# Causal masks of the second attention: added by VectorE to the diagonal blocks in PSUM, in place of products of bf16 mask rows

## The reference, cut to what matters

```python
scores = jnp.einsum('bhqd,bhkd->bhqk', q, k) * scale
causal = jnp.tril(jnp.ones((s, s), dtype=bool))
scores = jnp.where(causal, scores, -jnp.inf)
attn = jax.nn.softmax(scores, axis=-1)
ctx = jnp.einsum('bhqk,bhkd->bhqd', attn, v)
```

## Time and profile before

| what | us |
|---|---|
| median of 3 runs | 4223.27 |
| lowest and highest run | 4217.36, 4226.44 |
| the profiled execution | 4211.02 |
| span of its records | 4209.2 |
| busy in the span: PE | 3110.0 (74%) |
| PEld | 1905.6 (45%) |
| DVE | 2081.5 (49%) |
| ACT | 1452.4 (35%) |
| POOL | 588.3 (14%) |

### The profile page before, as it was taken

The page is one execution under the profiler, slowest core; times in us unless marked ns, Lnnn a source line. Parts: engine busy times, 40 slices in busy tenths (PEclk is TensorE's granted clock), DMA queues, the critical chain, the costliest instruction groups (busy, mean ns, idle before and its releaser), DMA issues. The chain is left out here.

```text
span 4209.2 us, 51448 instructions
## 1 busy us (share of the span) xinstructions
PE 3110.0 (74%) x17850; PEld 1905.6 (45%) x17850; DVE 2081.5 (49%) x3955; ACT 1452.4 (35%) x2880; POOL 588.3 (14%) x814
## 2 busy tenths in 40 slices
PE   2368879999999626999944559798344317999997
PEld 1134445555555323444433438788222214666664
DVE  3278766666666443333335558122555464333333
ACT  2246655555555422333343320000333222222222
POOL 2222115555555200000000000000100000000000
PEclk7679989999999858999965555667565558999998
DMA  1122200000000020000011123310000000000000
GB/s 57 54 54 37 42 26 4 4 4 4 4 4 1 18 67 19 14 14 5 0 46 33 51 74 101 86 45 15 4 0 0 0 0 15 15 7 7 7 7 20
DMA packets 145623, 101.46 MB, mean 24 GB/s; under 512 B 42616, under 2 KB 132587, under 8 KB 145115
## 3 DMA queue, kind: packets, MB, share of 16 engines
q1 hardware_dynamic: 145464, 99.35, 8.7%
HBM read 68.69 MB, written 30.63 MB: 24 GB/s over the span
## 5 line engine op out<-in xcount | busy, mean ns | idle before, releaser
L2320 ACT ACTIVATE f_silu<-f_g 128x512 f32<-128x512 f32 x256 | 152.9, 597 | 523.1 <-PE f_u L2298 523.1
L1274 DVE TENSOR_TENSOR x_hg<-x_h,x_g_ps 128x512 f32<-128x512 f32 x248 | 170.6, 688 | 328.9 <-PE x_y_ps L1219 296.9
L936 ACT ACTIVATE a_p<-a_s_ps,a_nmax 128x512 f32<-128x512 f32 (+3 forms) x512 | 268.1, 542 | 128.1 <-DVE a_nmax L852 128.1
L2345 DVE TENSOR_TENSOR f_act<-f_silu,f_u 128x512 f32<-128x512 f32 x256 | 176.1, 688 | 264.7 <-ACT f_silu L2320 264.7
L852 DVE TENSOR_REDUCE a_nmax<-a_s_ps 128x2 f32<-128x1024 f32 (+3 forms) x256 | 205.1, 822 | 168.9 <-PE a_s_ps L753 165.4
L1259 ACT ACTIVATE x_h<-x_h_ps,x_w 128x512 f32<-128x512 f32 x256 | 175.8, 687 | 323.6 <-PE x_g_ps L1215 296.2
L2297 PE MATMUL f_g<-hsT,f_wg 128*128 (+1 forms) x512 | 264.1, 597 | 28.9 <-DMA f_wd<-in_wd 17.0
L1211 PE MATMUL x_h_ps<-x_anT,x_w 128*128 128x512 f32 x512 | 263.1, 597 | 25.1 <-DMA x_gT<-gT_d 24.5
L910 POOL TENSOR_SCALAR a_p<-a_p,a_rden 128x512 f32<-128x512 f32 (+3 forms) x512 | 264.0, 536 | 12.1 <-DVE a_rden L859 11.9
L2298 PE MATMUL f_u<-hsT,f_wu 128*128 (+1 forms) x512 | 262.3, 594 | 0.0
L1219 PE MATMUL x_y_ps<-x_hg,x_w 128*128 128x512 f32 x496 | 253.1, 592 | 0.0
(11 more groups left out here) (408 smaller groups left out, 5522.8 us busy)
## 6 DMA issues: line engine op xcount, KB each, us to landing
l_band<-in_fir_long SPq DMA_DIRECT2D x16, 768.0 KB, 4.5
parts_d<-p_parts SPq DMA_DIRECT2D x16, 384.0 KB, 2.5
a_qs<-parts_d SPq DMA_DIRECT2D x96, 64.0 KB
a_ks<-parts_d SPq DMA_DIRECT2D x96, 64.0 KB
x_w<-in_w SPq DMA_DIRECT2D x8, 514.0 KB, 8.8
chan_d<-q_nT SPq DMA_DIRECT2D x16, 256.0 KB
p_xs<-in_x SPq DMA_DIRECT2D x8, 256.0 KB, 3.1
xfT_d<-p_xfT SPq DMA_DIRECT2D x8, 256.0 KB
```

What stands on the lines that cost most here:

```text
L936: last = nc.scalar.activation(p[g % 4][:, h, c:c + width(i)], s_ps[g % 2][:, h, c:c + width(i)], ACT.Exp, bias=nmax[g % 4][:, col], accum_ ...
L2345: nc.vector.tensor_tensor(act[s][:, f, :], g[f % 2][:, :], u_ps[f % 2][:, :], ALU.mult)\
```

## The change

In `scores` the products of mask rows are gone, and the last product of q and k signals `s_done`. In `maxima` VectorE adds the fp32 mask to each diagonal block of the step, in place in PSUM, for both heads with one instruction (128 partitions by 2 x 128 elements, the mask read twice by a stride of 0). A new semaphore `masked` counts these additions, and VectorE waits for its own additions before it takes the maxima. A pair has four additions (one, two and one in its steps) and three such waits; `MASKED` has the running count. Nothing else differs, and the first attention (`attn0`) keeps its products of mask rows.

```diff
--- before.py
+++ after.py
@@ -651,6 +651,7 @@
     n_pairs = NPAIR * B
     steps = 3 * n_pairs
     BLOCKS = (((3, 0),), ((2, 0), (0, 3 * P)), ((1, 0),))
+    MASKED = (1, 3, 4)
     with ExitStack() as ctx:
         sb = lambda name, shape, dt=F32: ctx.enter_context(nc.sbuf_tensor("a1_" + name, shape, dt))
         ps = lambda name, shape: ctx.enter_context(nc.psum_tensor("a1_" + name, shape, F32))
@@ -679,7 +680,7 @@
         s_done, max_ready, exp_done, rden_ready = sem("s_done"), sem("max_ready"), sem("exp_done"), sem("rden_ready")
         p_ready, pT_done, e_ready = sem("p_ready"), sem("pT_done"), sem("e_ready")
         ctx_done, cx_ready, o_done, oT_ready = sem("ctx_done"), sem("cx_ready"), sem("o_done"), sem("oT_ready")
-        y_done, acc_ready = sem("y_done"), sem("acc_ready")
+        y_done, acc_ready, masked = sem("y_done"), sem("acc_ready"), sem("masked")
         block = ctx.enter_context(nc.Block())
         halves = [slice(h * D1, (h + 1) * D1) for h in range(2)]
 
@@ -745,14 +746,8 @@
                 after(pe, exp_done, g - 1)
                 for at, (i, c) in enumerate(BLOCKS[g % 3]):
                     for h, hh in enumerate(halves):
-                        nc.tensor.matmul(out[:, h, c:c + width(i)], qT[s][hh, i * P:(i + 1) * P], kT[s][hh, 0:width(i)],
-                                         start=(at == 0), stop=False, skip_group_check=True)
-                for i, c in BLOCKS[g % 3]:
-                    for z in range(2):
-                        for h, hh in enumerate(halves):
-                            last = nc.tensor.matmul(out[:, h, c + i * P:c + width(i)], st["halfb"][hh, 0, z, :],
-                                                    st["halfb"][hh, 1, z, :], start=False, stop=z == 1,
-                                                    skip_group_check=True)
+                        last = nc.tensor.matmul(out[:, h, c:c + width(i)], qT[s][hh, i * P:(i + 1) * P], kT[s][hh, 0:width(i)],
+                                                start=(at == 0), stop=True, skip_group_check=True)
                 last.then_inc(s_done, 1)
 
             def transposes(g):
@@ -848,6 +843,10 @@
 
             def maxima(g):
                 v.wait_ge(s_done, g + 1)
+                for i, c in BLOCKS[g % 3]:
+                    diagonal = s_ps[g % 2][:, :, c + i * P:c + width(i)]
+                    nc.vector.tensor_tensor(diagonal, diagonal, bc(st["maskf"][:, 0, :], 2), ALU.add).then_inc(masked, 1)
+                v.wait_ge(masked, NB * (g // 3) + MASKED[g % 3])
                 for at, (i, c) in enumerate(BLOCKS[g % 3]):
                     last = nc.vector.tensor_reduce(nmax[g % 4][:, 2 * at:2 * at + 2], s_ps[g % 2][:, :, c:c + width(i)],
                                                    AX.X, ALU.max, negate=True)
```

## The result

The changed kernel takes 4237.94 us (median of 6 runs), the kernel before 4221.10 us (median of 6 in the same comparison). The ratio is 1.0042, with a 95% interval of 1.0029 to 1.0055: slower by 12 to 23 us. The forecast was 4238.

The account below looks back on a forecast made before the run. The prediction took a loop through several engines, not TensorE alone, as the bound: 11.94 to 12.22 us per pair. Repeating pairs +14.6, outputs -3.5 and ends +4 make +15 us, 4223.3 + 15 = 4238 us, range 4222 to 4270.

Parts of the forecast that it names:

- The bound: Per pair, two chains meet at step 1's exps: through the copy of v 11.94 us, through VectorE's maxima 11.72 us.
- chain of the copy: Loop through ScalarE's copy of v, which waits for v's projection: 11.94 us per pair, forecast to become 11.41.
- Step 1's additions: Two VectorE additions and a wait, less an earlier start, make step 1's maxima 0.76 + 0.04 - 0.09 = 0.71 us later.
- The removed products: TensorE's mask products: step 0's worth 0.21 us on both chains, step 1's 0.32 on the copy's only, step 2's nothing.
- VectorE's chain: Loop through VectorE's maxima of step 1: 11.72 us per pair, forecast 11.72 + 0.71 - 0.21 = 12.22 us.
- Steps 0 and 2 at nothing: One addition and wait each, 0.46 us on VectorE, covered by idle time and so costed at nothing.
- The wait: VectorE waiting for its own additions: next starts 0.04 us after the end, against 0.08 earlier without a wait.
- The outputs: Seven pairs that compute a sequence's output: TensorE's products count there, about -0.5 us each, -3.5 us together.
- The ends: First pairs and last four, where VectorE's chain stands bare: 0.5 to 0.8 us each, +4 us for both ends.
- The sum: Whole stage: 52 pairs +14.6 us, outputs -3.5, ends +4, together +15 us on the median of 4223.3.
- Rival D: TensorE's clock falls after 1.9 us idle per pair, 1.6 us a fall, giving 4266 to 4280 us; chance 0.20.
- Rivals A to C: TensorE's chain decides, 4192 or 4210 us, chance 0.06; a tie, 4224, 0.17; additions at upper end, 4268, 0.07.

Follow-up runs that it names:

- e1: Changed kernel with step 1's mask products back on TensorE, VectorE adding masks in steps 0 and 2 only; 4207.2 us, 0.9979 of the kernel before.
- e2: Changed kernel with VectorE adding step 0's mask only, steps 1 and 2 by products; 4213.3 us, 0.9989 of the kernel before.
- e4: Changed kernel with the additions left out too, so no causal mask in this attention; 4195.0 us, 0.9941 of the kernel before.
- e3: Changed kernel with VectorE adding step 1's two masks only, steps 0 and 2 by products; 4237.9 us, 1.0045 of the kernel before.
- e5: Changed kernel with step 1's two additions joined into one instruction of 128x512; 4244.9 us, one run.
- e6: Changed kernel with one mask addition and wait more, in step 0, 1 or 2 in turn; 4245.0, 4315.3 and 4244.5 us, one run each.
- e9: Changed kernel with one more wait, between step 1's two independent additions; 4286.3 us, one run.
- run 48: Not a label: "the one run 48 us slower" means e9's single run, 4286.3 us, with 48 a number of microseconds.

## Why the prediction was right

**The bound.** Two chains that meet at the exps of step 1, the one through the copy of v ahead by 0.22 us: shown. e1, e2 and e4 run on the chain of the copy, the changed kernel, e3, e5 and e6 on VectorE's. e1's one pair away from the outputs without a projection of v took 11.61 us beside its 11.83, the same 0.22.

**Step 1's additions: +0.71 forecast.** The parts, in the rows of the changed kernel: two additions and the wait from 915.81 to 916.59 are 0.78 us (0.80 forecast, 0.76 and 0.04), and the first starts 0.08 after the start of the reciprocal, at +3.19 and not +3.24 as taken, so it is a gain of 0.14 on the maxima's +3.33 (0.09 forecast). In all 0.64, so the forecast's 0.71 was 0.07 too high.

**The removed products: 0.21 for step 0, 0.32 for step 1.** These are the terms that were mis-sized; 0.11 and 0.22 were right. VectorE's chain shows the 0.11 by itself, in the pair just named: 11.72 before, 11.61 in e1. 0.64 - 0.11 = 0.53 on VectorE's chain of 11.72 gives 12.25, which was measured. The forecast's 12.22 is so close because two errors of 0.07 and 0.10, one on either side, nearly cancelled. In the chain through the copy of v nothing cancelled them: 11.94 - 0.11 - 0.22 = 11.61 is what e4 took, where the forecast had 11.41.

**Steps 0 and 2 at nothing.** Shown for a pair by e2 and by e6 in both steps.

**The wait: 0.12.** Measured at 0.13 (e9).

**The outputs: -0.5 each.** Measured -0.31, and not from the steps that were forecast. e3, without step 1's products, has 18.76 for 18.99, so these give 0.23. e2, without step 0's, has the same 18.98: they give nothing there. e1, without step 2's as well, has 18.90, which is the other 0.08. Why step 0's give nothing is argued, not shown: `values` waits for the addition of the output there (e6), behind the rotation of q, which step 2's products delay.

**The ends: +4 us.** Too low. The last four distances grew from 43.7 to 48.3 us, and the start, from the first projection to the first copy of `values`, by some 3.5 more, so 8 in all. Part is TensorE's clock, which now falls three times in the last pairs where it fell once; one of the three:

```profile
1430.73 1.09 PE L761 MATMUL a_pt_ps<-ident,a_p 128*128 128x128 f32 x4 [3.43 <-ACT a_e L945]
...
1431.75 2.08 PE L749 MATMUL a_s_ps<-a_kT,a_qT 64*128 64x512 f32 x4
```

These are the transposes after 3.43 us of idle time and the scores, 2.08 us for 1.13.

**The sum.** In the two profiled executions the stage grows by 52 x 0.30 = 15.7, less 2.2 for the outputs, plus 8 at the ends, 21.5 us, where 15 was forecast; the medians say 17 (12 to 23). The stage's growth was right to within some 6 us. That the total of 4238 came out to the tenth is luck: the three runs behind the 4223.3 that the sum started from lie 2.2 us above the median of six, and the errors in the terms cancelled in part.

**Rival D.** It was held at 0.20 and priced at 1.6 us a fall. The changed kernel is free of it: in mid-stage the clock stays at 1.00. But the mechanism is there at the price given, 14.3 - 12.72 = 1.6 us. My idle time of 1.9 us was too high, since it added the products at 0.74; by what they were worth (0.11 for each of steps 0 and 2, the latter from e1's and e2's idle times, and 0.22 for step 1) it is 0.90 + 0.30 + 0.44 = 1.64 us. In these profiles 1.65 us in each pair never brought a fall in mid-stage, and 1.77 did in half the pairs. Of e9's falls 28 are in mid-stage; with these, at 1.6 us each, the changed kernel would have taken about 4238 + 45 = 4283 us, outside the range. So the forecast held by a margin of 0.12 us of idle time or less. The rule cited from the Trainium skill, TensorE: Matmul & The Clock Gate, had only longer idle times as a danger. The changed kernel agrees with it; e9, whose clock falls behind 1.77 us, decides against it. Rivals A to C are out by the addition's 425 ns.

## What to carry to other kernels

Work that moves to an idle engine is paid by where it stands there, not by its share: the same addition with its wait cost 0 us a pair in steps 0 and 2 and 0.47 in step 1. So move the parts that have cover and leave the one that does not, which here (e1) is faster than either kernel, if only by 0.2% of the one before. And take a removed instruction's worth from its own length, not from the distance to the next row, unless the same pair of rows can be seen without it.

## What the runs showed of the hardware that was not expected

- The changed kernel stands close to a step. 0.13 us of delay per pair in the loop (e9, one wait) made the one run 48 us slower, not 8: TensorE's idle time went from 1.65 to 1.77 us, and the granted clock went to 0.50 behind it in half the pairs. The same idle time did it in one pair and not in the next.
- VectorE reads and writes PSUM in one instruction, in place, at the price of one that only reads it: 425 ns for 256 columns, on the line between 291 ns for 128 and 688 ns for 512, and 0.68 us for 512 (e5).
- Two bf16 products of 64 rows by 128 columns in the two halves of the array cost some 0.05 us together (12.25, 12.30 and 12.36 us with none, two and four).
